# One core, a recurrent layer with a gated feed-forward part: another order of the full step on all four compute engines

## What is computed

```
xn = layernorm(x)
# time mixing, per head: state S (64x64), token by token
sa = S @ a;  S = S * decay + outer(sa, b) + outer(v, k);  y = S @ r
s  = (groupnorm(y) * gamma + beta + bonus) * g @ oW.T
# r, w, k, v, a, g come from six mixtures of xn with its neighbour token
# feed-forward: top 2 of 8 experts, hidden = relu(xn @ wi.T + bi + lora_e)
out = x + s * silu(sum_e gate_e * (hidden_e @ wo.T + bo))
```

## Time and profile before

| | us |
|---|---|
| median of 3 runs | 990.77 (990.70 to 991.04) |
| the profiled execution | 991.04 |
| its span, first to last instruction | 989.2 |
| from one gram(0) to the next, most steps | 60.09 |

### The profile page before, as it was taken

How to read it: one execution, slowest core, us unless ns; L and a number is a source line. 1 busy time by engine, 2 the same in 40 slices (tenths; PEclk the granted TensorE clock), 3 DMA queues, 4 the chain that set the end, 5 groups by cost and what they waited for, 6 DMA issues and landing times.

```text
span 989.2 us, 46773 instructions
## 1 busy us (share of the span) xinstructions
PE 973.3 (98%) x20578; PEld 766.3 (77%) x20578; DVE 837.0 (85%) x1685; ACT 637.8 (64%) x1483; POOL 441.1 (45%) x536
## 2 busy tenths in 40 slices
PE   8999999999999999999999999999999999999997
PEld 5777778787787877777777787877878777787775
DVE  7988979789798897979979798897988979789776
ACT  4765765756757566676656667577575666756655
POOL 4452724427154361634627245372443716346150
PEclk9999999999999999999999999999999999999999
DMA  8000000000000000000000000000000000000000
GB/s 261 14 3 3 4 3 24 4 23 4 17 10 4 24 4 23 4 4 23 4 24 3 3 24 3 24 4 3 24 4 25 3 24 3 4 24 4 13 4 23
DMA packets 9416, 17.28 MB, mean 17 GB/s; under 512 B 1920, under 2 KB 4224, under 8 KB 8960
## 3 DMA queue, kind: packets, MB, share of 16 engines
q1 hardware_dynamic: 9216, 14.30, 4.5%
HBM read 10.10 MB, written 4.19 MB: 14 GB/s over the span
## 4 chain that ended last, share of the span: by engine, by line
PE 95%; DVE 2%; issue 1%; ACT 1%; SPq 0%; DMA 0%; ACTq 0%; DVEq 0%
PE bank L259 34%; PE bank L258 20%; PE grams L474 10%; PE bank L352 5%; PE bank L489 3%; PE bank L500 3%; PE grams L543 2%; PE grams L448 2%; PE grams L598 2%; PE grams L563 2%; PE bank L574 2%; PE bank L533 2%; PE bank L367 2%; PE bank L584 1%; PE bank L383 1%; PE bank L307 1%
## 5 line engine op out<-in xcount | busy, mean ns | idle before, releaser
L1272 POOL TENSOR_TENSOR bk<-bk,tot 128x256 f32<-128x256 f32 x192 | 155.4, 817 | 138.1 <-PE grams L474 138.1
L1594 DVE COPY_PREDICATED gm<-c_mask_g,grams 128x1024 f32<-128x1024 int32 x96 | 161.3, 1680 | 5.7 <-PE grams L474 3.9
L1026 ACT ACTIVATE gl<-gm 32x128 f32<-32x128 f32 x320 | 99.1, 310 | 78.3 <-DVE gm L1594 72.1
L917 ACT ACTIVATE relu<-bank,prm 128x256 f32<-128x256 f32 x256 | 105.7, 472 | 36.7 <-PE bank L259 34.2
L1253 POOL TENSOR_TENSOR xd<-mtmp,xnc 128x512 f32<-128x512 f32 x95 | 121.1, 1276 | 13.1 <-DVE mtmp L1455 11.3
L474 PEld LDWEIGHTS grams<-ar,bk 64*64 64x64 f32 x6144 | 102.2, 134 | 19.5 <-issue 14.4
L259 PE MATMUL bank<-w_wo,hid 128*128 128x256 f32 x488 | 116.1, 386 | 0.0
L474 PE MATMUL grams<-ar,bk 64*64 64x64 f32 x6144 | 110.2, 220 | 0.0
L1604 DVE TENSOR_TENSOR ar<-ar,tot 128x512 f32<-128x512 f32 x96 | 92.5, 964 | 13.2 <-PE grams L474 13.2
L259 PEld LDWEIGHTS bank<-w_wo,hid 128*128 128x128 f32 x488 | 90.1, 190 | 13.1
L259 PE MATMUL bank<-xnc,w_wi 128*128 128x256 f32 x392 | 94.4, 384 | 0.9 <-ACT relu L917 0.9
(11 more groups left out here) (247 smaller groups left out, 2150.8 us busy)
## 6 DMA issues: line engine op xcount, KB each, us to landing
x_in<-x SPq DMA_DIRECT2D x16, 256.0 KB, 2.9
out<-out_t SPq DMA_DIRECT2D x15, 256.0 KB, 2.0
w_wi<-w_wi_dram SPq DMA_DIRECT2D x1, 1024.0 KB, 7.0
w_wo<-w_wo_dram SPq DMA_DIRECT2D x1, 1024.0 KB, 9.3
w_lora_B<-w_lora_B_dram SPq DMA_DIRECT2D x1, 512.0 KB, 8.2
w_x_B<-w_x_B_dram SPq DMA_DIRECT2D x1, 384.0 KB, 3.2
w_kW<-w_kW_dram SPq DMA_DIRECT2D x1, 256.0 KB, 4.4
w_rW<-w_rW_dram SPq DMA_DIRECT2D x1, 256.0 KB, 4.0
```

Source lines behind the costliest of these rows:

```text
L917: A(dst[:, p % 2, j * 256:(j + 1) * 256], ZB[p % 2][:, j * 256:(j + 1) * 256], ACT.Relu, bias=prm[:, P_BI + 2 * p + j:P_BI + 2 * p + j + 1 ...
L1026: A(gl[l % 2][o:o + 32, :, :, :].rearrange("p q g (c n m) -> p (q g c) n m", c=2, m=m), right(gm[o:o + 32, :, :, :, b, 0, 32 * k:32 * k + ...
L1272: tt(v, v, d, ALU.mult).then_inc(S(f"bk{k}_scaled"), 1)
L1594: run(v.copy_predicated(dst, msk.to_broadcast([128, 32, HALF // m, m]), src), "g_stored")
```

## The change

Only the order of the full step (and of step 2, which uses the same code) changes on PE, ACT, DVE and POOL, and with it the places of the waits for banks and which bank a result goes to. `r_` and `o_` use the 128x128 form in place of halves, `lora(2)` too; `lora(3)` and `diff(3)` go the other way. On POOL `bv_` moves to the front and `mixed(2)` behind `scale_bk(5, 0)`, `decay(1)` to the end. No helper is added or taken away. In step 17 two waits for banks change their names.

In the diff 20 leading spaces are cut from the lines of the orders. ACT's first hunk moves `relu(1, 0)` ahead of `pack_gram(0)`; ACT's hunk for the rest of the step follows behind the first "...", then POOL's and DVE's.

```
@@ -58,8 +58,8 @@
         for p in range(PAIRS)}
 POSTS = {"ysg_done", "fgate_done", "zt_mm", "zt_done", "o_mm", "o_read", "out_done", "out_stored"}
-USED_BY = {"xt": 3, "route": 4, "mix": 3, "wk_A": 4, "kW": 3, "wk_B": 4, "g_A": 3, "zt": 4, "norm": 3, "keys0":
-           4, "r": 3, "a_A": 4, "a_B": 3, "bonus": 4, "keys1": 3, "o": 4, "v": 3, "xmt": 4, "g_B": 3,
+USED_BY = {"xt": 3, "route": 4, "mix": 3, "wk_A": 4, "kW": 3, "wk_B": 4, "g_A": 3, "norm": 4, "r": 3, "keys0":
+           4, "zt": 3, "a_A": 4, "a_B": 3, "o": 4, "bonus": 3, "keys1": 4, "v": 3, "g_B": 4, "xmt": 3,
            "last_zt": 3}
 FIRST_USED_BY = {"xt": 0, "route": 2, "mix": 1, "wk_A": 5, "kW": 6, "wk_B": 0, "g_A": 2, "r": 1, "a_A": 5, "norm": 6,
            "g_B": 0, "a_B": 2, "xmt": 1, "v": 5, "bonus": 6}
@@ -745,15 +745,15 @@
     base(0)
 if front:
     if full:
+        pe.wait_ge(*till("xmt_done", 0))
+    xt_()
+if rec:
+    lora(0)
+    diff(1)
+    gram(1)
+if front:
+    if full:
         pe.wait_ge(*till("gate_done", 0))
-    xt_()
-if rec:
-    diff(1)
-    lora(0)
-    gram(1)
-if front:
-    if full:
-        pe.wait_ge(*till("xmt_done", 0))
     route(half=True)
     pe.wait_ge(*till("xnc_done", 1))
     mix()
@@ -770,8 +770,8 @@
     gram(2)
     inv_x(1)
     base(2)
-    lora(3)
     inv_off(1)
+    lora(2)
 if front:
     pe.wait_ge(*till("mx_0_done", 2))
     pe.wait_ge(*till("mx_1_done", 2))
@@ -779,19 +779,19 @@
 if rec:
     gram(3)
     inv_x(2)
+    lora(3, half=True)
 if front:
     pe.wait_ge(*till("mx_3_done", 2))
     wk_A()
 if rec:
-    lora(2, half=True)
-    inv_off(2)
+    diff(2, half=True)
 if front:
     pe.wait_ge(*till("mx_2_done", 2))
     pe.wait_ge(*till("hwk_done", 1))
     miu(2)
 if rec:
     gram(4)
-    diff(3)
+    inv_off(2)
 if front:
     pe.wait_ge(*till("mx_4_done", 2))
     kW()
@@ -802,97 +802,100 @@
     wk_B()
 if rec:
     inv_off(3)
-    gram(5)
-    inv_x(4)
+    down(1, first=True)
 if front:
     pe.wait_ge(*till("kraw_done", 1))
     pe.wait_ge(*till("ksq_done", 1))
     g_A()
+if rec:
+    inv_x(4)
+    gram(5)
+    inv_off(4)
+if front:
+    pe.wait_ge(*till("sig_done", 2))
+    norm()
+    pe.wait_ge(*till("hg_done", 1))
+    r_()
+if rec:
+    top_x()
+    rec_p(0)
+    top_off()
+    if front:
+        pe.wait_ge(*till("nrm_done", 1))
+    elif full:
+        pe.wait_ge(*till("gate_done", 0))
+    keys_to_tokens(0)
 if post:
     if front:
-        pe.wait_ge(*till("sig_done", 2))
+        pe.wait_ge(*till("r_done", 1))
     elif full:
         pe.wait_ge(*till("xmt_done", 0))
     zt_()
 if rec:
-    inv_off(4)
-if front:
-    pe.wait_ge(*till("hg_done", 1))
-    norm()
-if rec:
-    down(1, first=True)
+    y_state(0)
+    rec_sa(0)
+    diff(3, half=True)
+if front:
+    if rec:
+        pe.wait_ge(*till("bkt_done", 1))
+    else:
+        pe.wait_ge(*till("nrm_done", 1))
+    a_A()
+if rec:
+    rec_inc(0)
+    rec_y(0)
+if front:
     if post:
         pe.wait_ge(*till("zt_done", 1))
-    elif front:
-        pe.wait_ge(*till("sig_done", 2))
+    else:
+        pe.wait_ge(*till("r_done", 1))
+    a_B(half=True)
+if rec:
+    rec_p(1)
+if post:
+    if front:
+        pe.wait_ge(*till("ha_done", 1))
+    elif rec:
+        pe.wait_ge(*till("bkt_done", 1))
     elif full:
-        pe.wait_ge(*till("xmt_done", 0))
-    keys_to_tokens(0)
-    top_x()
-    rec_p(0)
-    top_off()
-if front:
-    pe.wait_ge(*till("nrm_done", 1))
-    r_(half=True)
-    if rec:
-        pe.wait_ge(*till("bkt_done", 1))
-    elif post:
-        pe.wait_ge(*till("zt_done", 1))
-    else:
-        pe.wait_ge(*till("sig_done", 2))
-    a_A()
-if rec:
-    rec_sa(0)
-    y_state(0)
-    diff(2, half=True)
-    rec_inc(0)
-if front:
-    pe.wait_ge(*till("r_done", 1))
-    a_B(half=True)
-if rec:
-    rec_y(0)
-    rec_p(1)
-    down(0)
+        pe.wait_ge(*till("gate_done", 0))
+    o_()
+if rec:
     rec_sa(1)
     y_state(1)
 if front:
-    pe.wait_ge(*till("ha_done", 1))
+    pe.wait_ge(*till("agate_done", 2))
     bonus_()
 if rec:
-    if front:
-        pe.wait_ge(*till("agate_done", 2))
-    elif full:
-        pe.wait_ge(*till("gate_done", 0))
+    if post:
+        pe.wait_ge(*till("o_read", 1))
+    elif front:
+        pe.wait_ge(*till("ha_done", 1))
+    else:
+        pe.wait_ge(*till("bkt_done", 1))
     keys_to_tokens(1)
     rec_y(1)
-if post:
-    if front:
-        pe.wait_ge(*till("bonus_done", 1))
-    elif rec:
-        pe.wait_ge(*till("bkt_done", 1))
-    else:
-        pe.wait_ge(*till("zt_done", 1))
-    o_(half=True)
+if front:
+    pe.wait_ge(*till("bonus_done", 1))
+    v_(half=True)
 if rec:
     rec_inc(1)
+if front:
+    diag(rec)
+if rec:
+    down(0)
+    down(3)
+    down(2, final=True)
 if front:
     if rec:
         pe.wait_ge(*till("bkt_done", 2))
-    else:
-        pe.wait_ge(*till("agate_done", 2))
-    v_(half=True)
-    diag(rec)
-if rec:
-    down(3)
-    down(2, final=True)
-if front:
-    if post:
+    elif post:
         pe.wait_ge(*till("o_read", 1))
     else:
-        pe.wait_ge(*till("bonus_done", 1))
+        pe.wait_ge(*till("ha_done", 1))
+    g_B()
+    pe.wait_ge(*till("v_done", 3))
     xmt_()
-    pe.wait_ge(*till("v_done", 3))
-    g_B()
                 if step == 1:
 wait_loaded(pe, 2)
 wait_loaded(pe, 3)
...
@@ -1191,52 +1194,53 @@
     exps()
 if rec:
     pack_gram(2)
+    relu(1, 2)
+if front:
+    hwk()
+if rec:
     relu(1, 3)
-if front:
-    hwk()
-if rec:
     pack_gram(3)
 if post:
     ysg_()
 if rec:
-    relu(2, 3)
+    relu(2, 2)
+if front:
+    kraw_()
+if rec:
     pack_gram(4)
 if front:
-    kraw_()
     sig_()
     hg()
+    nrm_()
+if rec:
+    copy_blocks()
+if front:
+    r_e()
+if rec:
+    p_out(0)
+    inv_last()
+    keys_out(0)
+    sa_out(0)
 if post:
     zt_e()
 if front:
-    nrm_()
-if rec:
-    copy_blocks()
-    keys_out(0)
-    inv_last()
-    p_out(0)
-    relu(1, 2)
-if front:
-    r_e()
-if rec:
-    sa_out(0)
-if front:
     ha()
-if rec:
-    relu(2, 2)
-if front:
     agate_()
 if rec:
+    relu(2, 3)
     p_out(1)
     sa_out(1)
+    keys_out(1)
     y_out()
-    keys_out(1)
     ysq_()
+if front:
+    ar0(rec)
+if rec:
     sd8_()
 if front:
     v_e(rec)
+    gate_(step)
     xmt_e()
-    ar0(rec)
-    gate_(step)
                 A(scratch[:, 1:2], eps[:, 0:1], ACT.Copy).then_inc(S("act_end"), 1)
             act.wait_ge(zeroed, NZ)
@@ -1346,50 +1350,47 @@
     outadd()
                 else:
 if rec:
+    bv_()
+    next_tot(0)
     scale_bk(0, 1)
-    next_tot(0)
     scale_bk(0, 0)
+    scale_bk(1, 1)
     next_tot(1)
-    scale_bk(1, 1)
-    bv_()
     scale_bk(1, 0)
+    scale_bk(2, 1)
+    next_tot(2)
     scale_bk(2, 0)
 if front:
     mixed(1)
-if rec:
-    next_tot(2)
-    scale_bk(2, 1)
-if front:
     mixed(0)
 if rec:
     next_tot(3)
     scale_bk(3, 0)
+    next_tot(4)
+    scale_bk(3, 1)
+if front:
+    mixed(3)
+    mixed(4)
+if rec:
+    scale_bk(4, 1)
+if front:
+    mixed(5)
+if rec:
+    next_tot(5)
+    scale_bk(4, 0)
+if front:
+    ksum_()
+if rec:
+    scale_bk(5, 1)
+    decay(0)
+    scale_bk(5, 0)
 if front:
     mixed(2)
-if rec:
-    scale_bk(3, 1)
-if front:
-    mixed(3)
-if rec:
-    scale_bk(4, 0)
-    scale_bk(4, 1)
-if front:
-    mixed(4)
-if rec:
-    next_tot(4)
-    next_tot(5)
-if front:
-    mixed(5)
-    ksum_()
-if rec:
-    scale_bk(5, 1)
-    scale_bk(5, 0)
-    decay(0)
-    decay(1)
-if front:
     bk1(rec)
 if post:
     outadd()
+if rec:
+    decay(1)
                 tt(scratchp[:, 1:2], eps[:, 0:1], eps[:, 0:1], ALU.add).then_inc(S("pool_end"), 1)
             for buf in ZEROED_LATE:
@@ -1807,77 +1808,77 @@
     xm_()
 if rec:
     store(1)
+if front:
+    first_expert()
+if rec:
     scale_ar(1)
     start_inverse()
-if front:
-    first_expert()
-if rec:
     hidden(1)
 if front:
+    mixed(0)
     mixed(1)
-    mixed(0)
 if rec:
     keep_x(1)
     scale_ar(2)
     store(2)
+    hidden(0)
     add_off(1)
 if front:
     mixed(3)
+if rec:
+    scale_ar(3)
+if front:
     mixed(2)
 if rec:
+    store(3)
     keep_x(2)
-    store(3)
-    scale_ar(3)
+if front:
+    mixed(4)
+if rec:
     add_off(2)
-if front:
-    mixed(4)
-if rec:
-    store(4)
 if front:
     mixed(5)
 if rec:
     scale_ar(4)
     keep_x(3)
-    hidden(0)
+    store(4)
+if front:
+    first_mask()
+if rec:
     add_off(3)
-    keep_x(4)
-    store(5)
-    scale_ar(5)
-if front:
-    decay_step(rec)
-if rec:
-    add_off(4)
-if front:
-    first_mask()
 if post:
     fgate_()
 if rec:
+    keep_x(4)
+    hidden(2)
+    store(5)
+    add_off(4)
+    scale_ar(5)
     keep_top()
 if front:
+    decay_step(rec)
+    second_expert()
     key_norm()
-    second_expert()
+if rec:
+    new_state(0)
+if front:
+    kh_()
     gate_sum()
-if rec:
-    new_state(0)
-if front:
-    kh_()
-if rec:
-    hidden(3)
-if front:
     expert_masks()
     dg2_()
-if rec:
-    hidden(2)
+if post:
+    o_read()
+if rec:
+    hidden(3)
 if front:
     bonus_e(rec)
     bk0(rec)
+if rec:
+    centre()
+if front:
```

(49 more changed lines are left out.)

9 lines of the change are left out of this document (3 added, 6 removed).

## The result

| | before | after |
|---|---|---|
| median | 990.9 us (4 runs, 990.70 to 992.97) | 1003.85 us (4 runs, 1003.24 to 1003.99) |
| profiled execution, its span | 991.04, 989.2 | 1003.73, 1001.9 |
| one gram(0) to the next, most steps | 60.09 | 60.91 |
| gram(0) of step 3 to that of step 17 | 846.05 | 858.57 |

The change is slower by a ratio of 1.0123 (1.0111 to 1.0136). The forecast was 998.3, with a range from 990.5 to 1001.5: right in its sign, too low by 5.5 us and outside its range. The granted clock is 1.0 in both.

What follows compares the result with a forecast made beforehand. PE, busy 98% of the span, was taken to bound the kernel. 14 x (0.11 + 0.30 + 0.45) = 12.0, less 4.8, plus 0.3, gives +7.5 us: 998.3 us, range 990.5 to 1001.5.

Steps and rivals of the forecast that it cites:

- Term 1: PE, full step: 37 changes of the array's tile instead of 36, +0.11 us per step, +1.5 us over 14 steps.
- Term 3: Start of the step: bv_ first on POOL delays DVE's scale_ar(0), so gram(1) starts later; +0.30 us per full step.
- Term 4: Before rec_p(0): POOL's mixed(2), issued 0.09 us ahead, holds up DVE's scale_ar(5); +0.45 us per step.
- The waits put at nothing: Other waits in the step, such as kW on mx_4 or diag on bk1: 0.3 to 0.75 us spare, no cost.
- A: Neither wait, at the step's start or before rec_p(0), binds: -2.9 us, 987.9 us; chance 0.18.
- B: Only the wait at the start of the step binds: +1.9 us, 992.7 us; chance 0.14.
- C: Only the wait before rec_p(0) binds: +3.1 us, 993.9 us; chance 0.12.
- D: A further wait with 0.3 us of spare binds by 0.2 us per step: 1001.1 us; chance 0.06 together with E.
- Term 2: PE's holes, read as late instruction blocks in the densest row of small matmuls, go: -4.8 us, of which +0.3 returns.
- Rival E: PE's holes have another cause than late instruction blocks and stay: +4.5 us on the forecast, 1002.8 us; chance 0.06 with D.

Runs made afterwards that it cites:

- three_undone: Changed kernel with POOL's bv_ back behind scale_bk(1, 1), mixed(2) behind ksum_, and scale_bk(0, 1) ahead of next_tot(0) again; 994.05 us.
- bv_back: Changed kernel with only POOL's bv_ put back behind scale_bk(1, 1); 998.5 us.
- al_before: Kernel before with 208 records of satisfied waits on PE, placed so no block boundary falls where the records before it run fast; 988.99 us, ratio 0.9979.
- before_two_moves: Kernel before with POOL's bv_ and next_tot(0) moved to the front and mixed(2) behind scale_bk(5, 0); 995.42 us.
- both_undone: Changed kernel with POOL's bv_ back behind scale_bk(1, 1) and mixed(2) moved behind ksum_; 996.07 us.
- after_shift128: Changed kernel with 128 satisfied waits on PE ahead of its first step, which moved block boundaries by 64 places; 1010.5 us.

## Why the prediction was right and wrong

- **Term 1, tile changes, +0.11 us a step: right in size.** three_undone leaves 60.20 - 60.09 = 0.11; that the tile changes are its cause is not shown.
- **Term 3, the start of the step, +0.30: right**, with 0.29 measured, but its working gave all of it to bv_. bv_ is 0.20; the swap of next_tot(0) and scale_bk(0, 1), which the working did not price, is 0.09. In bv_back next_tot(0) runs before gram(0) ends, so it no longer parts the two scale_bk, and DVE's two xn_ take 1.58 us in place of 1.36. scale_ar(0) ended at +2.35 (forecast 2.44) and store(0) at +6.20 (6.32).
- **Term 4, before rec_p(0), +0.45: right**, 0.42 measured, for the reason given, by the 0.09 us given.
- **The waits put at nothing: right.** No view of the plain step shows a further one, and the four parts add up: 0.11 + 0.09 + 0.20 + 0.42 = 0.82 = 60.91 - 60.09. Rivals A, B, C and D fall.
- **Term 2, the holes, -4.8 and +0.3: this step failed.** It should have been +1.0. "A block boundary must fall into its last quarter or just behind it to be late" took a block as late only if nearly all of it lies in the densest row, as if the next fetch began with the block. The traces say otherwise. In the holes of 0.4 us and more the fetch had begun 1 to 194 records into the block, and the first instruction of the new block ran 2.2 to 2.8 us behind its start, of which the packet takes 0.9 to 1.4. Counted off in order, packet against boundary, none of the 2300 boundaries in the 14 traces is crossed sooner than 2.16 us behind the start of its fetch, with a hole or without. Where PE arrived more than 2.9 us behind that start there was no hole. So the 148 fast records of step 8 are enough, down(1) and g_A ahead of a row do not help (there they are over before the fetch begins), and every such row counts. An edit deals the 14 steps' boundaries anew, and the sum is that of a draw. The term also counted on the wait before rec_p(0) to hide a hole in the densest row. It hides 0.4 us only: in steps 7, 8 and 13 PE is 1.4 to 1.6 us late behind such a hole, and 1.0 to 1.2 us behind rec_p(0).
- **Rival E** named 1002.8 us, the nearest number, for a cause that the runs refute: the holes are late instruction blocks, and they stayed.

The Trainium skill ("Runtime: NRT & Kernel Launch", Instruction fetch mechanics) says that fetching a block is mostly hidden. This case's traces agree for "mostly": in steps 3 to 16 of the kernel after PE crosses some 142 boundaries, and five of them show a hole. In a row of small products it is not always hidden, and here it cost 1.2 to 1.6 us at once. The prediction read this rule as speaking for another cause, and it was a statement of the same one.

Not settled: what lets a fetch begin. At one boundary (ahead of kW, in step 6) it began some 106 records into the block in all five traces of this order of PE without added waits; at another (ahead of norm, in step 7) between 48 and 130.

## What to carry to other kernels

When a steady loop is bound by one engine, split the time into the plain step and what single steps take beyond it. Here the first was forecast to 0.05 us from the order of each engine; the second depends on where 256-record boundaries of the instruction stream fall, changes with any edit, and two orders should be compared without it. An operation of POOL that is issued just ahead of a two-input operation of DVE holds that one up until its own end and half a us more. PE pays for it only where it arrives soon behind: the same place was free in the old order. A hole that no semaphore ends, inside a row of equal small matmuls, can be removed by moving the boundary, with a few waits among long matmuls; in al_before that was worth 1.7 us.

## What was not expected of the hardware

- The fetch of the next instruction block often begins late, up to 149 of 256 records into the present one in the kernel after (194 at one hole of before_two_moves), and its first instruction ran 2.2 to 2.8 us behind that in the holes of 0.4 us and more.
- A hole of 1.6 us was followed by 3.4 us at half the granted clock in both_undone. In three_undone a hole as long at the same instruction, which ended at 664.8 too, was not, and neither was the one of 1.6 us in after_shift128; three_undone's row of the windows view has 1.00:

```profile
665.00:669.00 4.00, 4.00 (x98) 2.91 (x90) 3.49 (x9) 0.58 (x3) 2.39 (x3) 1.00 0.02 4
```

- A satisfied wait is not free: 90 ns for each record of two waits at the start of the kernel, where nothing hides it, and next to nothing between long matmuls.
